# A four-stage transformer kernel on one core: the last norm of the attention moved into the next program, weight copies moved ahead on VectorE, and another order of work in the drain

## What is computed

```
x = x + tanh(g_xattn[0]) * _L0_xattn_ref(_layernorm(x), ctx_1024, ...)   # two attentions, then a dense feed-forward
x = x + tanh(g_ffn[0])   * _L0_ffn_ref(_layernorm(x), ...)               # 8 experts, each row goes to 2
x = x + tanh(g_xattn[1]) * _L1_xattn_ref(_layernorm(x), ctx_1024, ...)   # attention with rotary positions
x = x + tanh(g_ffn[1])   * _L1_ffn_ref(_layernorm(x), ...)               # 8 experts, each row goes to 1

x2 = layer_norm(x + x1, ln1_g, ln1_b)        # inside _L0_xattn_ref; x1, x3 are the two attentions
x4 = layer_norm(x2 + x3, ln2_g, ln2_b)       # the norm whose last sequence the change moves
x5 = relu(x4 @ ff_w1 + ff_b1) @ ff_w2 + ff_b2
return layer_norm(x4 + x5, ln3_g, ln3_b)
```

## Time and profile before

| what | us |
|---|---|
| median of 3 runs (lowest to highest) | 1419.33 (1418.34 to 1425.44) |
| the profiled execution | 1420.58 |
| its span in the trace | 1418.7 |
| PE busy (matmul) | 1217.6, 86% of the span |
| DVE busy | 771.6, 54% |
| ACT busy | 560.9, 40% |
| POOL busy | 503.2, 35% |
| mean DMA rate over the span | 110 GB/s |

### The profile page before, as it was taken

One profiled execution on the slowest core, in us unless ns is written; L12 is line 12 of the kernel. 1 busy time (PEld: TensorE's weight loads), 2 busy tenths in 40 slices (PEclk: granted clock), 3 DMA queues, 4 the chain that ended last, 5 costly groups with the idle time before them and its releaser, 6 DMA issues. The chain is left out here.

```text
span 1418.7 us, 27157 instructions
## 1 busy us (share of the span) xinstructions
PE 1217.6 (86%) x8465; PEld 972.0 (69%) x8520; DVE 771.6 (54%) x2819; ACT 560.9 (40%) x1349; POOL 503.2 (35%) x909
## 2 busy tenths in 40 slices
PE   4598989999996899898999999755687888589996
PEld 3376666777753688788889888633455555489995
DVE  4676766777772277853412121147787876443321
ACT  2265555666664222233233333211354546133331
POOL 3344444453534235421000000156765543333331
PEclk9799999999999899999999999966799989799998
DMA  5767885657520771111111010166455587511110
GB/s 118 172 154 189 205 200 143 152 154 159 143 63 1 272 259 42 38 46 46 34 35 38 31 38 31 57 151 140 112 136 106 95 275 230 177 32 39 44 33 7
DMA packets 126293, 155.92 MB, mean 110 GB/s; under 512 B 19499, under 2 KB 111801, under 8 KB 121276
## 3 DMA queue, kind: packets, MB, share of 16 engines
q1 hardware_dynamic: 113736, 122.68, 34.2%
q0 software_dynamic: 9792, 27.30, 6.1%
q10 hardware_dynamic: 2624, 4.19, 1.0%
HBM read 104.17 MB, written 52.32 MB: 110 GB/s over the span
## 5 line engine op out<-in xcount | busy, mean ns | idle before, releaser
L761 DVE CUSTOM_DVE_ANT_0 att_masked_scores<-att_S,Bm 128x256 bf16<-128x256 f32 x512 | 192.4, 419 | 71.7 <-PE att_S L507 59.3
L644 ACT ACTIVATE att_PT<-att_T 128x512 f32<-128x512 f32 x256 | 151.4, 595 | 99.5 <-PE att_T L526 90.6
L2419 ACT ACTIVATE moe_hT<-moe_H,moe_b 128x128 f32<-128x128 f32 x312 | 89.2, 369 | 195.5 <-PE moe_H L2334 194.2
L2334 PE MATMUL moe_H<-moe_aT,ff_w 128*128 128x128 f32 x1248 | 147.7, 277 | 8.4 <-DVE ff_w L2617 8.4
L2334 PEld LDWEIGHTS moe_H<-moe_aT,ff_w 128*128 128x128 f32 x1248 | 146.7, 194 | 11.7 <-DVE ff_w L2617 9.9
L2346 PE MATMUL moe_Z<-moe_W,moe_hT 128*128 x624 | 142.6, 381 | 0.8 <-DVE moe_z L2624 0.8
L1615 POOL DMA_INDIRECT L_W<-yd,dest x32 | 31.3, 979 | 279.8 <-POOLq L52 271.2
L2346 PEld LDWEIGHTS moe_Z<-moe_W,moe_hT 128*128 128x128 f32 x624 | 115.4, 190 | 15.5 <-issue 1.2
L2624 DVE TENSOR_TENSOR moe_z<-moe_Z,moe_b 128x256 f32<-128x256 f32 x39 | 16.5, 424 | 200.7 <-PE moe_Z L2346 200.7
L507 PE MATMUL att_S<-L_KS,L_QS 96*128 96x256 bf16 x512 | 99.8, 277 | 26.9 <-DMA L_KS<-att_k_dram 21.7
L526 PE MATMUL att_T<-L_QS,L_KS 99*128 99x256 bf16 x512 | 98.7, 273 | 4.8 <-issue 2.3
(11 more groups left out here) (460 smaller groups left out, 2384.4 us busy)
## 6 DMA issues: line engine op xcount, KB each, us to landing
moe_W<-in_L_ffn_W SPq DMA_DIRECT2D x16, 1024.0 KB, 13.6
xd<-zero SPq DMA_DIRECT2D x12, 1280.0 KB
L_W<-in_L_ffn_W POOLq DMA_DIRECT2D x12, 1024.0 KB, 9.3
att_q_dram<-att_pq SPq DMA_DIRECT2D x16, 384.0 KB
att_k_dram<-att_pk SPq DMA_DIRECT2D x16, 384.0 KB
L_QS<-att_q_dram SPq DMA_DIRECT2D x16, 384.0 KB
L_KS<-att_k_dram SPq DMA_DIRECT2D x16, 384.0 KB
moe_xs<-xd SPq DMA_DIRECT2D x39, 128.0 KB
```

Source lines behind the costliest of these rows:

```text
L644: nc.scalar.activation(PT[:, h % 8, :], bankT[h % 2][:, :], ACT.Exp).then_inc(exp_done, 1)
L761: ins = nc.vector.tensor_tensor_reduce(masked_scores[:, h % 2, u, :], bankS[h % 2][:, u * SEQ:(u + 1) * SEQ], masks[m // B][0][:, u * SEQ: ...
L2334: ins = nc.tensor.matmul(bankH[half][:, f * P:(f + 1) * P], w1s[:, cc, g * P:(g + 1) * P], xT[:, s % 2, cc * P:(cc + 1) * P], start=(cc == ...
L2419: ins = nc.scalar.activation(eT[:, s % 2, g * P:(g + 1) * P], bankH[half][:, f * P:(f + 1) * P], ACT.Relu, bias=b1[:, bass.ds(e * NF + g, 1)])
```

## The change

Three parts. (A) The attention program ends one beat earlier: `output_rows` of the last unit writes its un-normalised rows straight into Y, and the norm of that sequence is done at the start of the feed-forward program: DVE's norm first of all, ACT's root after `bring(0)`, POOL's gain and shift (`finish_last`) after `add_bias(0)`, with gain and shift rows loaded into `yT` by two new DMAs at the head of SP's queue. PE's `turn(7)` and ACT's `bring_router(0)` wait for it. In the attention program `add_bias` of the last unit moves ahead of the norm of the unit before. (B) At the start of the feed-forward program's slots, `expert_matrix(0)` moves ahead of `new_rows(6)`, `expert_matrix(1)` ahead of `rows(7)`, `expert_matrix(2)` ahead of `new_rows(7)`; `turn_router(6)` moves from before `turn_slot(0)` to behind `up_slot(0)`, and logits and ranking of sequence 6 move one slot later. (C) In the last program `turn_router(5)`, `logits(5)`, `bring_router(5)` and `top_expert(5)` move into the last beat; POOL scatters sequence 5 ahead of the inverse roots of unit 6 and gathers slot 0 ahead of those of unit 7; `output_rows(7)` moves ahead of `norm(6)`; the loads of experts 6 and 7 move from ACT's queue to SP's, behind the row numbers of the first four slots and behind `keep_rows(6)`.

```
@@ -395,7 +395,8 @@
         scores_of = lambda b, h: (b + 1, H // 2 + h) if h < H // 2 else (b + 2, h - H // 2)
-        BEATS = range(-4, M + 2)
+        BEATS = range(-4, M + 1)
+        normed_here = lambda m: 0 <= m < M - 1
@@ -718,13 +719,15 @@
                     parts(b + 3, 0)
-                if has(b - 2):
+                if b == M:
+                    add_bias(M - 1)
+                if normed_here(b - 2):
                     inverse_roots(nc, pool, t, moments, root_step, b - 2).then_inc(rooted, 1)
...
                     parts(b + 3, 1)
-                if has(b - 2):
+                if normed_here(b - 2):
                     gain_and_shift(b - 2)
-                if has(b - 1):
+                if has(b - 1) and b < M:
                     add_bias(b - 1)
@@ -799,7 +802,8 @@
                     dve.wait_ge(y_done, m - 1)
-                nc.vector.tensor_tensor(z[:, m % 2, :, :], bank_of("z", m)[:, :].rearrange("p (u d) -> p u d", u=NU), ybb[:, :, :],
+                dst = z[:, m % 2, :, :] if m < M - 1 else here(Y, m)
+                nc.vector.tensor_tensor(dst, bank_of("z", m)[:, :].rearrange("p (u d) -> p u d", u=NU), ybb[:, :, :],
                                         ALU.add).then_inc(emptied("z", m), 1)
@@ -829,7 +833,7 @@
                         queries(b + 3)
-                    if h == 1 and has(b - 2):
+                    if h == 1 and normed_here(b - 2):
                         row_stats(b - 2)
@@ -839,7 +843,7 @@
                         max_columns(b + 1)
-                    if h == 9 and has(b - 2):
+                    if h == 9 and normed_here(b - 2):
                         norm(b - 2)
@@ -868,13 +872,15 @@
         return [t for t in LAST_FILL.get(h, ())]
+    more = LAST_BEAT.get(h, ()) if b == B - 1 else ()
     units = [(k, QUADS * b + d if k == "o" else b + d) for k, d in TASKS.get(h, ()) + ROUTE_TASKS.get(h, ())]
     last = {"o": QUADS * B, "t": EARLY_SEQUENCES1 - 1, "l": EARLY_SEQUENCES1 - 1, "n": EARLY_SEQUENCES1 - 1}
-    return [(k, n) for k, n in units if 0 <= n < last.get(k, B)]
+    return more + tuple((k, n) for k, n in units if 0 <= n < last.get(k, B))
...
 ROUTE_TASKS = {1: (("l", -3),), 5: (("n", -3),), 13: (("t", -2),)}
-DRAIN_TASKS = ("t", 5), ("l", 5), ("o", 31), ("n", 5), ("a", 7), ("z", 7), ("t", 6), ("l", 6), ("t", 7), ("l", 7), ("n", 6), ("n", 7)
+LAST_BEAT = {11: (("t", 5),), 14: (("l", 5),)}
+DRAIN_TASKS = ("n", 5), ("o", 31), ("a", 7), ("z", 7), ("t", 6), ("l", 6), ("t", 7), ("l", 7), ("n", 6), ("n", 7)
@@ -1130,11 +1136,16 @@
             experts_here(0, NE - 2)
-            keep_rows(B - 2)
             sp.wait_ge(early_made, 1)
...
                 numbers(s)
+            keep_rows(B - 2)
+            sp.wait_ge(s_ready, ALL)
+            sp.wait_ge(st_ready, ALL)
+            load_expert(sp, NE - 2)
+            sp.wait_ge(pv_done, QUADS * M + 2)
+            load_expert(sp, NE - 1)
             experts_here(NE - 2, NE)
@@ -1390,6 +1401,8 @@
                         turn_context(b + 4)
+                    if b == M - 1 and h == 11:
+                        turn_router(EARLY_ONES - 1)
                     if h in TURN_AT and 0 <= turning < QUADS * M:
@@ -1398,13 +1411,13 @@
                         turn_router(b - 2)
+                    if b == M - 1 and h == 14:
+                        logits(EARLY_ONES - 1)
                     if h in PV_AT and 0 <= quad < QUADS * M:
                         values(quad)
-            turn_router(EARLY_ONES - 1)
             values(QUADS * M - 1)
-            logits(EARLY_ONES - 1)
+            rank(EARLY_ONES - 1)
             turn_out(QUADS * M - 1)
-            rank(EARLY_ONES - 1)
             turn_heads(M - 1)
@@ -1554,15 +1567,11 @@
                         bring_router(b - 2)
+                    if b == M - 1 and h == 12:
+                        bring_router(EARLY_ONES - 1)
                     if h in PV_AT and 0 <= quad < QUADS * M:
                         outputs(quad)
-            bring_router(EARLY_ONES - 1)
-            act.wait_ge(s_ready, ALL)
-            act.wait_ge(st_ready, ALL)
-            load_expert(act, NE - 2)
             outputs(QUADS * M - 1)
-            act.wait_ge(pv_done, QUADS * M + 2)
-            load_expert(act, NE - 1)
             probabilities(EARLY_ONES - 1)
@@ -1731,10 +1740,11 @@
                     scatter(b - 3)
+            scatter(EARLY_ONES - 1)
             inverse_roots(nc, pool, t, moments, root_step, M - 2).then_inc(rooted, 1)
-            scatter(EARLY_ONES - 1)
+            rows_in(0)
             inverse_roots(nc, pool, t, moments, root_step, M - 1).then_inc(rooted, 1)
-            for s in range(EARLY):
+            for s in range(1, EARLY):
                 rows_in(s)
@@ -2038,17 +2048,18 @@
                         expert_weights(b - 3)
+                    if b == M - 1 and h == 15:
+                        top_expert(EARLY_ONES - 1)
+                        centre(EARLY_ONES - 1)
                     if h in TURN_AT and 0 <= turning < QUADS * M:
...
             row_stats(M - 2)
-            top_expert(EARLY_ONES - 1)
-            centre(EARLY_ONES - 1)
+            destinations(EARLY_ONES - 1)
             normalise(QUADS * M - 1)
-            destinations(EARLY_ONES - 1)
             expert_weights(EARLY_ONES - 1)
             early_table()
+            output_rows(M - 1)
             norm(M - 2)
-            output_rows(M - 1)
             row_stats(M - 1)
@@ -2210,6 +2221,7 @@
         w1_ready, x_loaded, y_stored = sem("w1_ready"), sem("x_loaded"), pair("y_stored")
+        last_in, last_normed, last_scaled, last_done = sem("last_in"), sem("last_normed"), sem("last_scaled"), sem("last_done")
         block = ctx.enter_context(nc.Block())
@@ -2224,6 +2236,8 @@
+            for i, k in enumerate(("last_gain", "last_shift")):
+                sp.dma_start(yT[:, i, :], rows_in[k].partition_broadcast(P)).then_inc(last_in, 16)
             for k in ("b2r", "gain", "shift"):
@@ -2252,6 +2266,8 @@
                     pe.wait_ge(t_out, n)
+                if n == B - 1:
+                    pe.wait_ge(last_done, 1)
                 for cc in range(NC):
@@ -2358,7 +2374,7 @@
                 down(n)
-                if n >= 1:
+                if 1 <= n < B - 1:
                     turn_router(n - 1)
@@ -2367,10 +2383,11 @@
                 if s == 0:
+                    turn_router(B - 2)
+                if s == 1:
                     logits(B - 2)
-                if s == 1:
+                if s == 2:
                     rank(B - 2)
-                if s == 2:
                     turn_router(B - 1)
@@ -2399,6 +2416,8 @@
                 act.wait_ge(r_turned, n + 1)
+                if n == 0:
+                    act.wait_ge(last_done, 1)
                 if n >= 1:
@@ -2422,12 +2441,13 @@
             bring(0)
+            norm_root(nc, act, t1, step1, root1, 0)
             for n in range(B):
...
                 if n >= 1:
-                    norm_root(nc, act, t1, step1, root1, n - 1)
+                    norm_root(nc, act, t1, step1, root1, n)
                 for j in range(1, HB):
@@ -2437,8 +2457,7 @@
             bring_slot(0)
-            bring_router(B - 2)
-            norm_root(nc, act, t1, step1, root1, B - 1)
+            norm_root(nc, act, t1, step1, root1, B)
             for s in range(SLOTS):
@@ -2447,6 +2466,8 @@
                     bring_slot(s + 1)
+                if s == 0:
+                    bring_router(B - 2)
                 if s == 2:
@@ -2458,6 +2479,13 @@
                 nc.gpsimd.tensor_tensor(here(Y, n), here(Y, n), rows_of(row_w["b2r"]), ALU.add).then_inc(ybb_done, 1)
+
+            def finish_last():
+                pool.wait_ge(last_in, 32)
+                pool.wait_ge(last_normed, 1)
+                nc.gpsimd.tensor_tensor(here(Y, B - 1), here(Y, B - 1), rows_of(yT[:, 0, :]), ALU.mult).then_inc(last_scaled, 1)
+                pool.wait_ge(last_scaled, 1)
+                nc.gpsimd.tensor_tensor(here(Y, B - 1), here(Y, B - 1), rows_of(yT[:, 1, :]), ALU.add).then_inc(last_done, 1)
@@ -2477,6 +2505,7 @@
             add_bias(0)
+            finish_last()
             for n in range(1, B + 1):
@@ -2507,7 +2536,7 @@
                 dve.wait_ge(z_out, n + 1)
-                norm_rows(nc, dve, z, z, t1, step1, root1, n, waited).then_inc(normed, 1)
+                norm_rows(nc, dve, z, z, t1, step1, root1, n + 1, waited).then_inc(normed, 1)
@@ -2624,31 +2653,36 @@
+            norm_rows(nc, dve, here(Y, B - 1), here(Y, B - 1), t1, step1, root1, 0, waited).then_inc(last_normed, 1)
             then(routing_constants(nc, rt))
...
                     top_experts(n - 2)
+                if n == B - 1:
+                    expert_matrix(0)
                 new_rows(n - 1)
...
             dve.wait_ge(b_loaded, 32)
-            expert_matrix(0)
+            expert_matrix(1)
             rows(B - 1)
...
                     dve.wait_ge(late_made, 1)
-                if s + 1 < SLOTS:
```

(12 more changed lines are left out.)

110 lines of the change are left out of this document (72 added, 38 removed).

## The result

| | before | changed |
|---|---|---|
| median | 1419.33 us (1416.5 to 1427.94, 9 runs) | 1410.85 us (1404.56 to 1418.19, 9 runs) |
| ratio to before, 95% interval | | 0.9924 [0.9903, 0.9944] |
| a second comparison | 1420.60 us (11 runs) | 1409.36 us (6 runs), 0.9920 [0.9897, 0.9943] |
| profiled execution, its span | 1420.58, 1418.7 us | 1414.69, 1412.6 us |

The changed kernel is faster by 0.76%, which is 10.8 us of 1419.33 (7.9 to 13.8); the medians differ by 8.5 us. The profiled execution is 5.9 us shorter, less than either, and part of the study was to find which of the numbers holds. The page of the profile shows nothing of it: PE is busy for 86% of the span as before. The places of single rows do.

What follows compares the result with a forecast made beforehand. PE, busy for 86% of the span, was taken as the bound, so only its waits pay. -10.5 (A) + 2.7 (B) - 3.0 (C) = -10.8 us took the median from 1419.33 to 1408.5 us, range 1403.5 to 1414.5.

Steps and rivals of the forecast that it cites:

- Part A, -10.5 us: End of attention: ends with POOL's shift of unit 14 at 455.00 instead of 465.54; bounds -11.5 and -9.5 us.
- The cover: Start of feed-forward program: the moved norm fits idle gaps there; without any cover it would cost 5.1 us.
- rival 3: Part C gains more and part A's first products start warm: a further -3 us, 1405.5; chance 0.13.
- Part B, +2.7 us: First feed-forward slots: slot 1's wait moves from DVE's copy to ACT's root, +1.1 us, plus a clock loss of +1.6.
- The clock's term: Slot 1's product in the feed-forward program: PE's longer idle stretch halves its clock, +1.6 us, bounds 0 and 2.0.
- Rival 1: No clock loss in part B's first slots, so 1.6 us less, 1406.9; chance 0.17.
- Part C, -3.0 us: Drain of the last program: faster scatter and row numbers outweigh later expert weights; bounds -4.5 and +2 us.
- scatter issued: Drain: expert_weights, for which the scatter waits, ends at 1210.85 instead of 1209.79, +1.05 us, bounds 0 and +2.5.
- scatter lands: Drain: without expert loads beside it the scatter lands after 4.5 instead of 7.30 us, -2.8, bounds -3 and 0.
- row numbers: Drain: the load of row numbers takes the usual 1.8 instead of 3.21 us, -1.4, bounds -1.5 and 0.
- if the first slots of the last program wait for their rows: Drain of the last program: a sign named as showing the prediction wrong; no size given.
- Rivals 2, 4 and 5: Drain gains nothing, 1412.7, chance 0.13; late expert loads delay slot 4, 1422, 0.03; part A's norm cover fails, 1413.6, 0.06.

Runs made afterwards that it cites:

- e6_root_late: Changed kernel with ACT's root for the last sequence's norm moved behind hidden_slot(0), bring_slot(1) and bring_router(6); ratio to the kernel before 0.9917.
- e2_copies: Kernel before with part B alone, the early copies of the first slots' matrices; ratio to the kernel before 1.0018.
- e3_drain: Kernel before with part C alone, the new order in the last program's drain; ratio to the kernel before 0.9984.
- e4_norm_drain: Changed kernel without part B, so parts A and C; ratio to the kernel before 0.9896.
- e8_router_13: Parts A and C without B, with turn_router(5) put behind project_out(6) instead of ahead of it; ratio to the kernel before 0.9895.

## Why the prediction was right, point by point

The forecast was 1408.5 us with -10.8 us; measured were 1410.85 us as a median, -10.8 us by the ratio and -11.4 in the second comparison. The time lies where it was put, and the three mechanisms are those of the prediction. That both numbers read 10.8 is luck: the interval is 7.9 to 13.8 us, the medians differ by 8.5, and by the traces B cost more and C gave less than forecast, so that the three parts come to 8 to 10 us.

**Part A, -10.5 us: right,** by the mechanism and in the trace (10.55; 10.2 to 10.6 between any two traces). The cover held: the first relu was not delayed, and PE did not wait at the eighth sequence's turn, turn(7). What the prediction left to rival 3, products that start at full clock, came true in four of eleven traces, and is worth 0.5 to 0.9 us there, too little to explain why A alone measures -12.1; the interval of that run is too wide to need a reason.

**Part B, +2.7 us: right in the mechanism, too small in one term.** The wait moved from DVE's copy to ACT's root and slot 1 came 1.1 us later (140.4 against 139.3), as worked out; e6_root_late shows that the root is the cause. The clock's term is the mis-sized one. The prediction took 1.6 us, from a product that had followed a wait of 2.40 us, with 2.0 as the bound; measured are 6.34, 6.36 and 6.70 us against 3.84, so 2.5 to 2.9 us, the clock being half for 5 us of the product. By the distance to slot 2 part B costs 3.3 us (151.2 - 147.9), by the distance to the last program 3.3 and 3.6 us, by time 2.6 us (0.3 to 4.7). Alone, in e2_copies, it costs 4.4 and 4.5 us by the same distances. Rival 1, no clock loss, is out. What the forecast could not see from one trace is that the old order has such a loss too in some executions: behind the same wait of 2.43 us the product of slot 0 took 3.84 us in four of the kernels without B, 5.28 in two and 6.75 in one. Part of it is covered there: slot 1 then starts at 139.9 and 141.2 us instead of 138.5 to 139.3.

**Part C, -3.0 us: right in direction, -2.5 and -2.6 us at slot 4 in two traces, but -1.7 in e3_drain and -0.55 in the first trace of the changed kernel; by time -2.3 us (-5.1 to +0.4).** Its terms against what the two traces of the changed kernel and e4_norm_drain show:

| term | prediction | measured |
|---|---|---|
| project_out(6) | +1.8 | +1.4 |
| scatter issued | +1.05 | +0.4 (28.16 us behind project_out(5) instead of 27.74) |
| scatter lands | -2.8 | -3.1 (4.1 to 4.2 us) |
| row numbers | -1.4 | -1.4 |
| gather of slot 0, issue to PE's turn | 0 | +0.2 and +0.6, once +3.3 |
| slot 0's product at half clock | 0 | -0.1, +0.2 and +0.8 (4.74, 5.04 and 5.61 us against 4.80) |
| slot 1 | +0.1 | +0.45 and +1.04 of waiting for its rows, once 0 |
| from project_out(5) to slot 4 | -3.0 | -2.6, -2.5, once -0.55 |

The term that was mis-sized is the one on the loads' new place: "the expert loads begin about 2 us behind the gather and meet that of slot 1, which has about 3 us to spare". They do meet it, and it takes 3.7 us longer, so the 3 us to spare are used up. Slot 0's product, which the sum took to stay as it was, is the second one. From slot 4's product to the last one it takes 136.7 us before and 137.4 and 137.5 in the two traces of the changed kernel; in the chain a gather of 3.2 us behind a store of rows of 5.3 us stands there in both. But e3_drain, e4_norm_drain and e8_router_13, with the same loads and gathers, have 136.7 us, so it isn't shown to be the price of part C. One sign that the prediction named for being wrong did come, "if the first slots of the last program wait for their rows": PE still waits 8.10 us for slot 0's rows (13.01 before) and, in the second trace, 1.04 us for slot 1's. Its own sum had only shortened the first of these waits.

**Rivals 2, 4 and 5** did not come: the scatter gained in all kernels that moved the loads, slot 4 never waited for its row numbers, the cover in A held. The two spans of the first profiles differ by 6.1 us, and the marks say where: -10.55 us up to the feed-forward program, +3.3 up to the last program, +0.9 from there to project_out(5), -0.55 to slot 4 and +0.8 behind it. The gather of 7.34 us is 2 of the missing us. The +0.9 lies in a stretch that the change hardly touches and that takes 258.6 to 263.1 us in the fourteen traces.

**A version that is faster than both by all that was measured** is the changed kernel without part B: 1403.49 us as a median against 1410.85, 0.9896 [0.9868, 0.9923] to before. Against the changed kernel the intervals overlap; that it is better rests on the 3.3 us and more of part B which each trace shows, and on the three other kernels with A and a form of C but no B, at 0.9895 to 0.9902. Those with B and one or both roots late have 0.9917, 0.9920, 0.9916 and 0.9896.

## What to carry to other kernels

When a copy is moved earlier to free a wait, list for the engine that then becomes last (here ACT) everything that stands ahead of its part in program order: an instruction that waits there for a third engine passes its wait on. Curing one such wait showed the next: ACT's first root, its second root, then DVE's wait for POOL ahead of new_rows(7). DVE was not full there (busy for 15.76 of 26.99 us), nor ACT (9.26 us), so adding up their work would not have shown it; write out the order and the waits instead. Bulk loads cost the small transfers beside them 2.3 to 3.7 us each in both places tried; look for a stretch in which no such transfer is waited for. And when one profile is to carry a sum of a few us, read distances between fixed marks in several traces, because a single execution was off by some 3 us in one gather here.

## What the runs showed of the hardware that I had not expected

- TensorE's clock after a wait: 1.00 us of idle time left it at 2.4 GHz (3.81 us for 32 matmuls of 128x128); after 2.43 us the same product took 3.84, 5.28 or 6.75 us; after 4.68 us (two traces) the clock fell to 1.2 GHz 0.4 us into the product, which took 5.44 us; after 5.75 us (three traces) it had fallen before the product began, which took 6.3 to 6.7 us. So the same short wait cost 0, 1.4 or 2.9 us in slot 0's product, without anything in the program to choose between them. At the seventh slot of that program a wait of 2.3 to 2.5 us cost 1.5 to 1.6 us (5.30 to 5.47 us) in ten traces and nothing in three. The Trainium skill ("TensorE: Matmul & The Clock Gate", Part 1: The HAM clock gate) calls the count of slow matmuls at a kernel's start variable from run to run; these rows show the same inside a kernel.
- A gather of 128 rows of 2 KB takes 3.3 to 3.8 us with little else moving and 7.1 to 7.5 us beside 4 MB of loads at about 380 GB/s; the scatter of row numbers takes 3.7 to 4.2 and 6.5 to 7.3 us.
- DVE's copy of an expert's matrix takes 1.23 us and POOL's gain of sequence 7 1.26 us. Where the two began within 0.04 us of each other, one of them took 1.1 us longer: the gain 2.35 us in the changed kernel (595.73), the copy 2.31 us before (604.01).
- The attention's last product took 2.0 us in eight of the traces and 3.3 to 3.8 us in six. The first transpose behind it came 5.8 to 5.9 us after the product's start all the same where the norm had moved, since POOL and DVE set the program's end.
